# Pairwise products of 200 field vectors in fp32: TensorE's program as a loop over eight groups, and mixed rows moved by GpSimd and VectorE

## The chip, the cores and the metric

One NeuronCore of a Trainium2 chip. The metric is the device time of one execution in microseconds (us), the median of a few runs.

## The reference

Everything is fp32. There are 512 samples, each with 200 fields of 64 numbers, and a 64 x 64 weight matrix for every field.

```python
B, F, E = (256, 200, 64)            # r_feature is (512, 200, 64)
bilinear = jnp.einsum('bie,ied->bid', feature, weight)
out = jnp.einsum('bid,bjd->bij', bilinear, feature)
```

So every field i of a sample is first multiplied by its own matrix ("mixed"), and then the 200 x 200 products of mixed and plain field vectors of each sample are formed ("scores"). 82 MB of scores are written, 26 MB of features read.

## The kernel before

The samples are worked in 4 groups of 128. The 128 partitions hold two halves: partitions 0 to 63 the 64 numbers of one half of a group's samples, 64 to 127 those of the other half; the weights stand twice, once for each half (w_sb).

**Mixes.** A mix unit (L200) is 32 matmuls of a 64 x 64 weight with 64 moving columns (one column a sample) into a pair of PSUM banks, four tiles of 64 x 64 side by side in the array. The fields are taken in three chunks of 64 (four mix units each), and the last 8 fields ("tail") in a unit of their own (L217). In a mix unit one bank gets its result in the own half of the partitions, the other in the opposite half; ScalarE and VectorE copy them from PSUM into mixed (L293, and L291 for the bank that changes halves, in two copies of 64 partitions).

**Scores.** A score unit (L228) is 8 matmuls: for 8 samples the 64 mixed fields of a chunk are the stationary operand and all 200 plain fields of the sample, straight from x_sb, the moving one; again four tiles of 64 x 64 side by side. It fills a pair of banks, 128 x 800 numbers, which ScalarE (even units) or VectorE (odd units) copies to a slot of tile (L270); two units make an output of 128 x 1600 that SyncE (SP) sends (L154). tile has 6 slots. The tail's scores are two more units a group (L244) of 64 matmuls with 32 columns each.

**Order.** walk (L36) sets one order of units for all engines. The mix units of the next chunk stand between the score units of the present one. Four bank pairs go round, so a unit waits for the copy of the unit four before (wait_banks). TensorE, ScalarE, VectorE and SP each run their whole program unrolled. SP sends the outputs in order, and in between, one or two output issues apart, the loads of the next group: part 0 during chunk 0 into the other of two buffers, part 1 during the last chunk into the single buffer piece by piece (L155 to L162). GpSimd does one memset (L168).

In the recorded instructions every fp32 matmul shows as two MATMUL and two LDWEIGHTS.

## Time and profile before

| | |
|---|---|
| median of 3 runs | 349.12 us (348.49 to 352.26) |
| the profiled execution | 347.19 us, its span 345.4 us |
| TensorE (PE) busy | 250.5 us, 73% of the span |
| VectorE (DVE), ScalarE (ACT), GpSimd (POOL) busy | 148.4, 128.3 and 2.4 us |
| mean granted TensorE clock | 0.93 of full speed |
| moved by DMA | 115.70 MB, mean 335 GB/s |

The span is from the first to the last instruction of the profiled execution; what lies around it is 1.8 us. A line number in a row is that of the listing above. "<-" stands between a tile that is written and the one read, or ahead of what released an engine. PEld is the load of weights. "Issue" is time in which an engine waited for nothing that the profile shows. PEclk is given in tenths of full speed in the slices (9 is 0.9 or more), as a fraction in the windows; 1.00 is 2.4 GHz and half of it is 1.2 GHz.

### The profile page before, as it was taken

How to read it: one execution, taken by the hardware profiler on the slowest of the kernel's cores; microseconds unless marked ns; L12 is line 12 of the kernel's file. 1: busy time of each engine (PE TensorE's matmuls, PEld its weight loads, DVE VectorE, ACT ScalarE, POOL GpSimd, SP SyncE). 2: the span in 40 equal slices, each digit the busy share in tenths (PEclk: the TensorE clock that was granted, in tenths of full speed). 3: DMA queues.
4: the chain of work that ended last, by engine and by line, in shares of the span. 5: the costliest groups of instructions: out<-in, count | busy, mean ns of one | idle time of the engine just before them, and what ended most of it. 6: DMA issues, size and time to landing. Idle time of an engine off the chain costs nothing.

```text
span 345.4 us, 15674 instructions
## 1 busy us (share of the span) xinstructions
PE 250.5 (73%) x7296; PEld 221.2 (64%) x7296; DVE 148.4 (43%) x172; ACT 128.3 (37%) x177; POOL 2.4 (1%) x5
## 2 busy tenths in 40 slices
PE   0167679599967674969785967869985877987870
PEld 0156668378867573748775957748875766766760
DVE  0042455136634541605563553504653554635550
ACT  1032426045524422314452443403553444442540
POOL 2000000000000000000000000000000000000000
PEclk9987899899989988989998798989999999999995
DMA  7999998847999997757799999964899997746796
GB/s 302 423 426 423 400 368 280 331 193 289 351 409 399 395 388 261 236 242 291 300 374 418 395 366 421 306 286 194 335 373 390 407 386 312 289 199 260 284 408 286
DMA packets 21808, 115.70 MB, mean 335 GB/s; under 512 B 2416, under 2 KB 2416, under 8 KB 21360
## 3 DMA queue, kind: packets, MB, share of 16 engines
q1 hardware_dynamic: 21744, 114.70, 84.6%
q8 instruction: 58, 0.95, 1.1%
q14 instruction: 6, 0.05, 0.0%
HBM read 32.77 MB, written 81.92 MB: 332 GB/s over the span
## 4 chain that ended last, share of the span: by engine, by line
PE 72%; issue 19%; DMA 4%; DVE 1%; SPq 1%; ACT 1%
PE psum L238 46%; PE psum L210 16%; PE psum L255 9%; DMA w_sb<-w_dram 4%; PE psum L222 1%; DVE tile L270 1%; SPq L128 1%; ACT mixed L291 1%
## 5 line engine op out<-in xcount | busy, mean ns | idle before, releaser
L238 PE MATMUL psum<-x_sb,mixed 64*64 64x200 f32 x3072 | 173.2, 357 | 32.9 <-issue 29.5
L238 PEld LDWEIGHTS psum<-x_sb,mixed 64*64 64x64 f32 x3072 | 141.4, 143 | 49.5 <-issue 41.2
L270 DVE COPY tile<-psum 128x800 f32<-128x800 f32 x100 | 99.2, 992 | 141.2 <-PE psum L238 128.9
L270 ACT COPY tile<-psum 128x800 f32<-128x800 f32 x100 | 82.7, 827 | 117.2 <-PE psum L238 85.5
L210 PE MATMUL psum<-x_sb,w_sb 64*64 64x64 f32 x3072 | 67.7, 228 | 37.3 <-issue 21.3
L210 PEld LDWEIGHTS psum<-x_sb,w_sb 64*64 64x64 f32 x3072 | 65.6, 140 | 40.6 <-issue 39.5
L291 DVE COPY mixed<-psum 64x512 f32<-64x512 f32 x48 | 33.1, 689 | 28.2 <-PE psum L210 26.9
L291 ACT COPY mixed<-psum 64x512 f32<-64x512 f32 x48 | 27.9, 581 | 43.6 <-PE psum L210 43.0
L255 PE MATMUL psum<-x_sb,tails 64*32 64x200 f32 x1024 | 32.6, 377 | 13.0 <-issue 13.0
L255 PEld LDWEIGHTS psum<-x_sb,tails 64*32 64x32 f32 x1024 | 22.6, 115 | 21.7 <-issue 18.3
L293 ACT COPY mixed<-psum 128x512 f32<-128x512 f32 x24 | 14.1, 587 | 44.3 <-PE psum L210 44.2
L293 DVE COPY mixed<-psum 128x512 f32<-128x512 f32 x24 | 16.6, 692 | 17.6 <-PE psum L210 17.6
L222 PE MATMUL psum<-x_sb,w_sb 64*64 64x64 f32 x128 | 4.6, 220 | 0.5
L222 PEld LDWEIGHTS psum<-x_sb,w_sb 64*64 64x64 f32 x128 | 4.2, 132 | 0.9 <-issue 0.9
L300 ACT COPY tails<-psum 128x512 f32<-128x512 f32 x4 | 2.3, 586 | 0.3
L168 POOL MEMSET tails<- 128x2560 f32 x1 | 2.2, 2232 | 0.3 <-POOLq L324 0.3
L293 ACT ACT_TABLE_LOAD x1 | 1.3, 1283 | 0.7 <-PEq L324 0.7
L324 POOL MEMSET const-bfloat16-1.0<- 128x1 bf16 x1 | 0.1, 103 | 0.0
L324 POOL MEMSET const-uint8-127<- 128x1 uint8 x1 | 0.1, 102 | 0.0
L324 POOL MEMSET const-float32-0.0<- 128x1 f32 x1 | 0.1, 100 | 0.2 <-issue 0.2
L324 POOL MEMSET const-float32-1.0<- 128x1 f32 x1 | 0.1, 100 | 0.0
## 6 DMA issues: line engine op xcount, KB each, us to landing
out_dram<-tile SPq DMA_DIRECT2D x96, 800.0 KB, 6.3
x_sb<-x_dram SPq DMA_DIRECT2D x16, 800.0 KB, 8.7
x_sb<-x_dram SPq DMA_DIRECT2D x32, 400.0 KB, 7.7
w_sb<-w_dram SPq DMA_DIRECT2D x2, 2048.0 KB, 16.7
out_tail_dram<-tile SPq DMA_DIRECT2D x4, 800.0 KB, 4.5
w_sb<-w_dram SPq DMA_DIRECT2D x1, 2304.0 KB, 22.5
```

Source lines behind the costliest of these rows:

```text
L128: eng.dma_start(x_sb[:, 2 * (g % 2), quads], x[g, 0, :, quads]).then_inc(part0_loaded[g % 2], 16)
L168: nc.gpsimd.memset(tails[:], 0.0).then_inc(zeroed, 1)
L210: last = nc.tensor.matmul(psum[half_rows(h ^ swap), bank + swap, r * HALF_SAMPLES:(r + 1) * HALF_SAMPLES], w_sb[half_rows(h), field, :], x ...
L222: last = nc.tensor.matmul(psum[half_rows(h), n % BANK_PAIRS * 2, r * HALF_SAMPLES:(r + 1) * HALF_SAMPLES], w_sb[half_rows(h), TAIL_FIRST + ...
L238: last = nc.tensor.matmul(psum[half_rows(pair), n % BANK_PAIRS * 2 + h, a * FIELDS:(a + 1) * FIELDS], mixed[half_rows(h), (CHUNKS * g + c) ...
L255: last = nc.tensor.matmul(psum[tile4 * TAIL_TILE:(tile4 + 1) * TAIL_TILE, n % BANK_PAIRS * 2 + h, piece * FIELDS:(piece + 1) * FIELDS], we ...
L270: copy(tile[:, k % SLOTS, engine], psum[:, bank:bank + 2, 0:2 * FIELDS]).then_inc(copied[engine], 1)
L291: copy(to[half_rows(h)], source[half_rows(1 - h)]).then_inc(copied[engine], 1)
L293: copy(to, source).then_inc(copied[engine], 1)
L300: copy(tails[:, :, :, 0:TAIL], source).then_inc(copied[engine], 1)
L324: nc = bacc.Bacc("TRN2", target_bir_lowering=False, num_devices=1)
```

## The change

There are now 8 groups of 64 samples. The halves of the partitions no longer divide the samples but the fields: partitions 0 to 63 hold fields 0 to 103 of all 64 samples, partitions 64 to 127 fields 104 to 199 (96 fields and 8 rows of zeros). The weights are loaded once, split alike.

A mix unit is 32 matmuls as before (two units have 16, the last 8); its results go to made, one ScalarE copy a unit (L299). To score, all 200 mixed fields of a sample must stand in both halves. So made is copied to mixed in eight steps of 8 samples: VectorE copies all partitions straight across into fields 0 to 99 (L309), and GpSimd, in two copies of 64 partitions, the rows that change halves into fields 100 to 199 (L195). GpSimd also copies x_in, which lies field by field, to x_now, which lies sample by sample (L188), in eight steps.

A score unit has 2 samples: x_now with 104 or 96 columns is the stationary operand, the 200 mixed fields the moving one (L230), so two matmuls, one a half, stand side by side. ScalarE copies 5 units of 8, VectorE 3. Two units make an output of 96 x 1600 and one of 8 x 800 (L158, L159); tile has 4 slots. The tails are gone.

x_in is a single buffer: SP loads the next group right after the first output of a group (in the first group after the fourth), when GpSimd has copied all of x_in (x_placed) and the mixes have read it. TensorE's program is a loop of 7 rounds (L251), one group's 32 score units and the next group's 8 mix units, with the semaphore values in registers; the last group stands behind the loop. The other engines stay unrolled.

```diff
-GROUPS = 4
-HALVES = 2
-QUADS = BATCH // GROUPS // 4
-HALF_SAMPLES = 2 * QUADS
+GROUPS, SLOTS = 8, 64
+MAIN, REST = 96, 8
+TOP = MAIN + REST
+PIECES = 3
+PIECE = MAIN // PIECES
+MIX = [(16 * m, 8, 2) for m in range(5)] + [(80, 4, 2), (88, 4, 2), (MAIN, 4, 1)]
+MIXES = len(MIX)
+MADE = FIELDS // 2
...
+MIX_AFTER = (7, 9, 12, 14, 17, 20, 22, 24)
+STEPS = 8
+STEP_SLOTS = SLOTS // STEPS
+STEP_UNITS = STEP_SLOTS // UNIT_SAMPLES
+NEXT_STEPS_AFTER = {28: 0, 30: 1}
+STEPS_AFTER = {STEP_UNITS * n + 2: n + 2 for n in range(STEPS - 2)}
+POOL_STEPS = [("x", c) for c in range(6)] + [("rows", 0), ("x", 6), ("rows", 1), ("x", 7)]
+POOL_STEPS += [("rows", c) for c in range(2, STEPS)]
+TILE_UNITS = 2
+TILES = SCORES // TILE_UNITS
+TILE_SLOTS = 4
...
+def engine_of(u):
+    return 0 if u % 2 == 0 or u % 8 == 7 else 1
...
-def build(nc, x, weight, out, out_tail):
-    sb = lambda name, shape: nc.alloc_sbuf_tensor(name, shape, F32)
-    w_sb = sb("w_sb", [128, FIELDS, EMB])
-    x_sb = sb("x_sb", [128, 3, QUADS, PART, 2])
-    mixed = sb("mixed", [128, 2, QUADS, CHUNK, 2])
+    w_sb = sb("w_sb", [128, TOP, EMB])
+    x_in = sb("x_in", [128, TOP, SLOTS])
+    x_now = sb("x_now", [128, SLOTS, TOP])
+    made = sb("made", [128, 2, SLOTS, MADE])
+    mixed = sb("mixed", [128, SLOTS, FIELDS])
+    tile = sb("tile", [128, TILE_SLOTS, 2, TILE_UNITS, UNIT_SAMPLES * FIELDS])
...
         def _(sp):
...
+            for p in range(PIECES + 1):
+                load_x(0, p)
+                load_w(p)
+            for g in range(GROUPS):
+                for t in range(TILES):
+                    k = g * TILES + t
+                    s = k % TILE_SLOTS
+                    for u in range(TILE_UNITS * t, TILE_UNITS * (t + 1)):
+                        e = engine_of(u)
+                        sp.wait_ge(copied[e], COPIES[NUMBER["score", g, u]][e])
+                    sp.dma_start(out[g, t], tile[0:MAIN, s]).then_inc(slot_out[s], 16)
+                    sp.dma_start(out_rest[g, t], tile[MAIN:TOP, s, 0]).then_inc(slot_out[s], 16)
+                    if g + 1 < GROUPS and t == (3 if g == 0 else 0):
+                        sp.wait_ge(x_placed, STEPS * (g + 1))
+                        sp.wait_ge(unit_ready, NUMBER["mix", g, MIXES - 1] + 1)
+                        for p in range(PIECES + 1):
+                            load_x(g + 1, p)
...
         def _(pool):
-            nc.gpsimd.memset(tails[:], 0.0).then_inc(zeroed, 1)
+            nc.gpsimd.memset(x_in[half_rows(1), MAIN:TOP, :], 0.0).then_inc(zeroed, 1)
+            pool.wait_ge(zeroed, 1)
+            for g in range(GROUPS):
+                for p in range(PIECES + 1):
+                    pool.wait_ge(x_loaded[p], 16 * (g + 1))
+                for step in POOL_STEPS:
+                    what, c = step
+                    slots = slice(c * STEP_SLOTS, (c + 1) * STEP_SLOTS)
+                    if step == ("rows", 0):
+                        pool.wait_ge(copied[0], COPIES[NUMBER["mix", g, MIXES - 1]][0])
+                    if g > 0 and what == "x":
+                        pool.wait_ge(unit_ready, NUMBER["score", g - 1, (c + 1) * STEP_UNITS - 1] + 1)
+                    if g > 0 or crossed_before(step):
+                        pool.wait_ge(crossed, 2 * (STEPS * g + crossed_before(step)))
+                    if what == "x":
+                        nc.gpsimd.tensor_copy(
+                            x_now[:, slots, :], x_in[:, :, slots].rearrange("p f s -> p s f")).then_inc(x_placed, 1)
+                    else:
+                        pool.wait_ge(x_placed, STEPS * g + min(STEPS, 6 + c))
+                        for h in range(2):
+                            if h == 1:
+                                pool.wait_ge(crossed, 2 * (STEPS * g + c) + 1)
+                            nc.gpsimd.tensor_copy(mixed[half_rows(h), slots, MADE:FIELDS],
+                                                  made[half_rows(1 - h), g % 2, slots, :]).then_inc(crossed, 1)
...
         def _(pe):
...
+            def mix(n, m):
+                first, width, banks = MIX[m]
+                bank = n % BANK_PAIRS * 2
+                for r in range(width):
+                    for swap in range(2):
...
+                            last = nc.tensor.matmul(
+                                psum[half_rows(h ^ swap), bank + (swap if banks == 2 else 0),
+                                     r * SLOTS:(r + 1) * SLOTS],
+                                w_sb[half_rows(h), field, :], x_in[half_rows(h), field, :],
+                                start=True, stop=True)
+                last.then_inc(unit_ready, 1)
-                wait_banks(n)
-                if t == 0 and u == 0:
-                    wait_copies(NUMBER["mix", g, c, MIX_UNITS - 1])
-                if c == 0 and u == 0:
-                    wait_part1(g, t)
-                for a in range(2):
-                    quad = 4 * t + 2 * u + a
-                    for pair in range(2):
-                        for h in range(HALVES):
-                            last = nc.tensor.matmul(
-                                psum[half_rows(pair), n % BANK_PAIRS * 2 + h, a * FIELDS:(a + 1) * FIELDS],
-                                mixed[half_rows(h), (CHUNKS * g + c) % 2, quad, :, pair],
-                                x_sample(g, h, quad, pair), start=True, stop=True)
+            def score(n, u):
+                bank = n % BANK_PAIRS * 2
+                for a in range(UNIT_SAMPLES):
+                    slot = UNIT_SAMPLES * u + a
+                    for h, rows in enumerate((TOP, MAIN)):
+                        last = nc.tensor.matmul(
+                            psum[0:rows, bank + h, a * FIELDS:(a + 1) * FIELDS],
+                            x_now[half_rows(h), slot, 0:rows], mixed[half_rows(h), slot, :], start=True, stop=True)
+                last.then_inc(unit_ready, 1)
+            def wait_step(g, u):
+                if u % STEP_UNITS == 0:
+                    steps = u // STEP_UNITS + 1
+                    pe.wait_ge(x_placed, g * STEPS + steps)
+                    pe.wait_ge(mixed_placed, g * STEPS + steps)
+                    pe.wait_ge(crossed, g * (2 * STEPS) + 2 * steps)
+            with pe.Fori(0, GROUPS - 1) as g:
+                x_there = 16 * g + 32
+                pe.compute_val(x_there)
+                for kind, to, k in order(1):
+                    n = NUMBER[kind, to, k]
+                    (free, value), = banks_free(n, g)
+                    pe.compute_val(value)
+                    if kind == "mix":
+                        pe.wait_ge(w_loaded[piece_of(k)], 16)
+                        pe.wait_ge(free, value)
+                        pe.wait_ge(x_loaded[piece_of(k)], x_there)
+                        mix(n, k)
+                    else:
+                        pe.wait_ge(free, value)
+                        wait_step(g, k)
+                        score(n, k)
...
         def copies(eng, copy, engine):
...
+                    eng.wait_ge(slot_out[k % TILE_SLOTS], 32 * (k // TILE_SLOTS))
+                bank = n % BANK_PAIRS * 2
+                copy(tile[0:TOP, k % TILE_SLOTS, :, u % TILE_UNITS, :],
+                     psum[0:TOP, bank:bank + 2, 0:UNIT_SAMPLES * FIELDS]).then_inc(copied[engine], 1)
...
+            def place(g, c):
+                if c == 0:
+                    eng.wait_ge(copied[0], COPIES[NUMBER["mix", g, MIXES - 1]][0])
+                if g > 0:
+                    eng.wait_ge(unit_ready, NUMBER["score", g - 1, (c + 1) * STEP_UNITS - 1] + 1)
+                slots = slice(c * STEP_SLOTS, (c + 1) * STEP_SLOTS)
+                copy(mixed[:, slots, 0:MADE], made[:, g % 2, slots, :]).then_inc(mixed_placed, 1)
+            if engine == 0:
+                for m in range(MIXES):
+                    mix(0, m)
+            else:
+                for c in NEXT_STEPS_AFTER.values():
+                    place(0, c)
+            for g in range(GROUPS):
+                for kind, to, k in order(g):
+                    if kind == "mix":
+                        if engine == 0:
+                            mix(to, k)
+                        continue
+                    if engine_of(k) == engine:
+                        score(g, k)
+                    if engine == 1 and k in STEPS_AFTER:
+                        place(g, STEPS_AFTER[k])
+                    if engine == 1 and k in NEXT_STEPS_AFTER and g + 1 < GROUPS:
+                        place(g + 1, NEXT_STEPS_AFTER[k])
```

How the instructions stand. First TensorE in the middle of a group, before. L238 is a score matmul, L210 a mix matmul, L255 one of the tail; x_sb is the input, mixed the mixed fields.

```order
L238 MATMUL psum<-x_sb,mixed 64x200 [waits copied_dve]
L238 MATMUL psum<-x_sb,mixed 64x200 x7
L238 MATMUL psum<-x_sb,mixed 64x200 [waits copied_act]
L238 MATMUL psum<-x_sb,mixed 64x200 x7
L255 MATMUL psum<-x_sb,tails 32x200 [waits copied_act,copied_dve,zeroed]
L255 MATMUL psum<-x_sb,tails 32x200 x63
L238 MATMUL psum<-x_sb,mixed 64x200 [waits copied_dve,copied_act]
L238 MATMUL psum<-x_sb,mixed 64x200 x7
L238 MATMUL psum<-x_sb,mixed 64x200 [waits copied_act]
L238 MATMUL psum<-x_sb,mixed 64x200 x7
L210 MATMUL psum<-x_sb,w_sb 64x64 [waits part1_loaded3,part1_loaded2,part1_loaded4,part1_loaded1,part1_loaded5,part1_loaded0,part1_loaded6,w_loaded2,part1_loaded7,part0_loaded0,copied_dve]
L210 MATMUL psum<-x_sb,w_sb 64x64 x31
```

After, units 6 and 7 of a group, the first mix unit of the next group, and unit 8. L230 is a score matmul, L218 one of a mix; L257, L239 and L241 are register and wait instructions.

```order
L230 MATMUL psum<-mixed,x_now 104x200 [waits copied_dve]
L230 MATMUL psum<-mixed,x_now 96x200
L230 MATMUL psum<-mixed,x_now 104x200
L230 MATMUL psum<-mixed,x_now 96x200
L257 REGISTER_ALU
L218 MATMUL psum<-x_in,w_sb 64x64 [waits x_loaded0,copied_act,w_loaded0]
L218 MATMUL psum<-x_in,w_sb 64x64 x31
L257 REGISTER_ALU
L239 REGISTER_ALU [waits copied_dve]
L241 REGISTER_ALU [waits mixed_placed,x_placed]
L230 MATMUL psum<-mixed,x_now 104x200 [waits crossed]
```

The first mix unit now waits for x_loaded0, the first piece of the next group, which before was loaded one chunk or more earlier; between the units stand register instructions.

SP (SyncE), before, at the end of a group: outputs (L154) and the loads of the next group (L132).

```order
L154 DMA out_dram<-tile 128x1600 [waits copied_dve,copied_act] x5
L154 DMA out_tail_dram<-tile 128x1600 [waits copied_dve,copied_act]
L154 DMA out_dram<-tile 128x1600 [waits copied_dve,copied_act] x4
L132 DMA x_sb<-x_dram 128x800
L154 DMA out_dram<-tile 128x1600 [waits copied_dve,copied_act]
L132 DMA x_sb<-x_dram 128x800
L154 DMA out_dram<-tile 128x1600 [waits copied_dve,copied_act]
```

After, at the start of the second group: the outputs are L158 and L159, the loads L137 and L139.

```order
L158 DMA out_dram<-tile 96x1600 [waits copied_act]
L159 DMA out_rest_dram<-tile 8x800
L158 DMA out_dram<-tile 96x1600 [waits copied_dve,copied_act]
L159 DMA out_rest_dram<-tile 8x800
L137 DMA x_in<-x_dram 128x2048 [waits unit_ready,x_placed]
L137 DMA x_in<-x_dram 128x2048 x2
L139 DMA x_in<-x_rest_dram 64x512
L158 DMA out_dram<-tile 96x1600 [waits copied_dve,copied_act]
L159 DMA out_rest_dram<-tile 8x800
```

The loads stood singly between outputs; now all of a group's loads stand behind its first output, behind a wait for GpSimd (x_placed) and TensorE (unit_ready).

GpSimd, before, from its start to its end.

```order
L166 UNCONDITIONAL_BRANCH [waits barrier_Pool_Activation_PE_DVE_SP_gather]
L168 MEMSET tails 128x2560
L134 UNCONDITIONAL_BRANCH
```

After, in the second group, from the end of the x steps on (L188 copies x_in to x_now, L195 rows that change halves).

```order
L188 COPY x_now<-x_in 128x832 [waits crossed,unit_ready] x5
L195 COPY mixed<-made 64x8x100 [waits x_placed,crossed,copied_act]
L195 COPY mixed<-made 64x8x100 [waits crossed]
L188 COPY x_now<-x_in 128x832 [waits crossed,unit_ready]
L195 COPY mixed<-made 64x8x100 [waits x_placed,crossed]
L195 COPY mixed<-made 64x8x100 [waits crossed]
L188 COPY x_now<-x_in 128x832 [waits crossed,unit_ready]
L195 COPY mixed<-made 64x8x100 [waits x_placed,crossed]
L195 COPY mixed<-made 64x8x100 [waits crossed]
```

Before, GpSimd had no copy at all; now each of its copies waits for the one before, and the x steps also for the score units of the group before (unit_ready).

## Rows read from the trace of the kernel before

**Rows 1.** The page: busy shares; 40 equal slices of PE (tenths) and DMA (GB/s).

```profile
PE 250.5 (73%) x7296; PEld 221.2 (64%) x7296; DVE 148.4 (43%) x172; ACT 128.3 (37%) x177; POOL 2.4 (1%) x5
...
PE   0167679599967674969785967869985877987870
...
GB/s 302 423 426 423 400 368 280 331 193 289 351 409 399 395 388 261 236 242 291 300 374 418 395 366 421 306 286 194 335 373 390 407 386 312 289 199 260 284 408 286
```

**Rows 2.** The page: chain that ended last.

```profile
PE 72%; issue 19%; DMA 4%; DVE 1%; SPq 1%; ACT 1%
```

**Rows 3.** Waits of TensorE: who waited for what, us in total, times, longest.

```profile
PE psum L238 <- issue: 29.5, 17, 4.5
PE psum L210 <- issue: 21.3, 14, 3.1
PE psum L210 <- DMA w_sb<-w_dram: 16.0, 1, 16.0
PE psum L255 <- issue: 13.0, 6, 3.9
```

**Rows 4.** The page: instruction queue; issues, us to landing; then all x_sb loads.

```profile
q8 instruction: 58, 0.95, 1.1%
...
out_dram<-tile SPq DMA_DIRECT2D x96, 800.0 KB, 6.3
x_sb<-x_dram SPq DMA_DIRECT2D x16, 800.0 KB, 8.7
...
DMA to landing us min/median/max: 4.4/7.8/18.2
```

**Rows 5.** The page: groups of instructions.

```profile
L270 DVE COPY tile<-psum 128x800 f32<-128x800 f32 x100 | 99.2, 992 | 141.2 <-PE psum L238 128.9
L270 ACT COPY tile<-psum 128x800 f32<-128x800 f32 x100 | 82.7, 827 | 117.2 <-PE psum L238 85.5
...
L168 POOL MEMSET tails<- 128x2560 f32 x1 | 2.2, 2232 | 0.3 <-POOLq L324 0.3
...
L324 POOL MEMSET const-bfloat16-1.0<- 128x1 bf16 x1 | 0.1, 103 | 0.0
```

**Rows 6.** The chain in order of time, 150 to 165 us: start, us, what.

```profile
154.61 0.95 PE psum L210 x59
155.56 1.43 PE psum L238 x28
156.99 3.02 PE psum L255 x116
...
161.60 1.04 PE psum L210 x60
```

**Rows 7.** Timeline of the last stretch: start, us, what.

```profile
322.13 0.83 ACT L270 COPY tile<-psum 128x800 f32<-128x800 f32 x1 [1.73 <-PE psum L238]
...
333.62 0.83 ACT L270 COPY tile<-psum 128x800 f32<-128x800 f32 x1 [0.62 <-PE psum L238]
334.33 0.99 DVE L270 COPY tile<-psum 128x800 f32<-128x800 f32 x1 [0.44 <-PE psum L238]
```

**Rows 8.** Windows: busy of each engine, PEclk, DMA share, GB/s.

```profile
26.50:335.40 308.90, 243.77 (x7040) 214.69 (x7040) 144.23 (x166) 123.53 (x170) 0.00 (x0) 0.94 0.85 332
...
26.00:31.70 5.70, 5.12 (x89) 4.37 (x91) 1.14 (x2) 2.03 (x3) 0.00 (x0) 0.60 1.02 432
321.00:334.40 13.40, 13.15 (x288) 12.53 (x288) 8.00 (x9) 7.40 (x9) 0.00 (x0) 1.00 0.83 335
```

**Rows 9.** Timeline of the start.

```profile
0.73 2.06 SPq L128 DMA_DIRECT2D x_sb<-x_dram  x4
...
15.99 5.43 PE L210 MATMUL psum<-x_sb,w_sb 64*64 64x64 f32 x221 [15.99 <-DMA w_sb<-w_dram]
...
26.58 4.91 PE L238 MATMUL psum<-x_sb,mixed 64*64 64x200 f32 x64 [1.43 <-ACT mixed L291]
```

**Rows 10.** Waits of SyncE.

```profile
SPq L164 <- DMA out_dram<-tile: 9.1, 1, 9.1
```

More of the change, by code:

```diff
@@ L39, in half_rows, with crossed_before @@
+POOL_STEPS = [("x", c) for c in range(6)] + [("rows", 0), ("x", 6), ("rows", 1), ("x", 7)]
[3 more added lines that the diff above has]
+TILE_SLOTS = 4
+def crossed_before(step):
+    return sum(what == "rows" for what, _ in POOL_STEPS[:POOL_STEPS.index(step)])
 def half_rows(h):
     return slice(h * EMB, (h + 1) * EMB)
[L43 to L69 removed]
@@ new lines, in engine_of, with fields_by_position @@
+def engine_of(u):
+    return 0 if u % 2 == 0 or u % 8 == 7 else 1
+def fields_by_position():
+    made = [[], []]
+    for first, width, banks in MIX:
+        if first == MAIN:
+            for h in range(2):
+                made[h] += range(first + h * width, first + (h + 1) * width)
+        else:
+            for bank in range(banks):
+                for h in range(2):
+                    a = h * TOP + first + bank * width
+                    made[h ^ bank] += range(a, a + width)
+    return [made[h] + made[1 - h] for h in range(2)]
@@ new lines, in order @@
+def order(g):
+    for u in range(SCORES):
+        yield "score", g, u
+        if u in MIX_AFTER and g + 1 < GROUPS:
+            yield "mix", g + 1, MIX_AFTER.index(u)
+def count_copies():
+    copies, number = [], {}
+    units = [("mix", 0, m) for m in range(MIXES)] + [unit for g in range(GROUPS) for unit in order(g)]
+    a = d = 0
+    for n, (kind, g, k) in enumerate(units):
+        engine = 0 if kind == "mix" else engine_of(k)
+        a, d = a + (engine == 0), d + (engine == 1)
+        copies.append((a, d))
+        number[kind, g, k] = n
+    return copies, number
@@ L335 @@
[L335 to L342 removed]
+    r = run_bass_kernel_spmd(nc, [inputs], core_ids=[0]).results[0]
```

285 lines of the change are left out of this document (84 added, 201 removed).

## The prediction

> **What bounds the kernel now.** I read the page's busy line and its slices first, then the chain of waits, the waits of TensorE, the groups by line, clean stretches in the timeline, and the DMA part. TensorE is busy in 7 to 9 tenths of nearly every slice while VectorE and ScalarE stay near half, and the DMA rows are high but uneven, 193 to 426 GB/s [rows 1]. The chain that ended last runs 72% over TensorE and 19% over "issue" [rows 2]: 0.192 x 345.4 = 66 us in which TensorE waited for nothing that the profile shows. TensorE's own waits put 29.5, 21.3 and 13.0 us of such time before its three kinds of work, together 64 us, in 37 pieces of up to 4.5 us [rows 3]. Only instruction delivery fits: the instruction queue moved 58 packets, 0.95 MB [rows 4], for 2 x 7,296 TensorE instructions [rows 1], so 16 KB and about 250 instructions a packet; the pauses fall more thickly around mixes and tails, which use up instructions fastest. So TensorE bounds the kernel, partly starved of instructions; the DMA engines come second.
>
> **TensorE's work.** One unit is what one pair of banks takes. In a complete stretch a mix unit (64 recorded matmuls) stands for about 1.0 us (0.95 and 1.04), two score units for 1.43 us, a tail unit for 3.02 us [rows 6]; the last stretch, at clock 1.00, has ScalarE's copies from 322.13 to 333.62 in eight steps, 1.44 us for two score units, too [rows 7]. Before: 192 x 0.72 + 50 x 1.0 + 8 x 3.0 = 212 us. The chain shows 249 (72%), a factor of 1.17: cold stretches after pauses (clock 0.94 in the middle and 0.60 in one stretch, where the first four score units took 4.9 us instead of 2.9 [rows 8, 9]) and small handovers.
> After: a score unit holds 2 samples x 2 halves = 4 matmuls instead of 8, but they are 104 or 96 columns wide, so only two stand side by side instead of four. Half the matmuls at half the concurrency: 0.72 us again, but 256 units instead of 192. The tails go (-24 us). The mixes keep 3,200 recorded matmuls, 50 us. Sum 184 + 50 = 234, 22 us more than before. Of this 6 us (the first group's mixes) lie in the start. For the other 228 I take a factor of 1.12, between 1.05 (the last stretch, without pauses, is at 1.00; I allow 5% for handovers) and 1.17 (as before), since one kind of pause goes and another comes (below): 255 us, bounds 239 to 267.
>
> **Instruction pauses.** The body of the new loop is 128 score and 200 mix matmuls, 1,312 recorded instructions; by 65 bytes each 85 KB. If it stays in the engine, the 66 us go; if it is fetched again in every round, they stay in part. No row shows which. I take the first, since the body is a tenth of what the program was, and give the other as a rival. No row prices the register instruction that now stands ahead of each unit; the smallest instruction on the page takes 0.10 us [rows 5]. I cost them at 0, covered by matmuls already queued; uncovered, 0.1 us x 320 units = 32 us, of which the range holds half.
>
> **Loads of the next group.** Before, x of the next group is spread over output issues a chunk or more ahead, and TensorE's waits show no x load at all [rows 3]. Now x_in is single: SP issues all four loads after tile 0 of the group. That is 2 units, 1.4 us, a copy of 1.0 us and an issue, so 2.8 us into the group. The old 800 KB loads took a median of 8.7 us from issue to landing [rows 4]; the first mix wants its piece after eight units, 5.8 us in. Wait: 2.8 + 8.7 - 5.8 = 5.7 us; with the fastest landings (4.4 us) 1.4 us. I take 5 x 7 groups = 35 us, bounds 10 to 45. Queued behind the waiting matmul are all later score units; the copies run dry after 4 bank pairs. Behind SP's wait for x_placed stand the outputs; that wait ends once GpSimd has moved x step 7, which itself waits for the last score unit of the group before.
>
> **GpSimd and VectorE.** Per group GpSimd gets 8 copies of 832 elements and 16 of 800. The only row of it is the memset, 2,560 elements in 2,232 ns, 0.87 ns an element, write only [rows 5]: at this floor 8 x 0.73 + 16 x 0.70 = 17 us a group. If reading takes as long again, 34 us. TensorE's group is (23 + 6.2) x 1.12 + 5 = 38 us, so up to 34 it is hidden but for the start. I take 1.4 us for an x step (its reads are strided) and 1.0 for a row copy with its semaphore: 27 us. VectorE: 12 x 0.99 + 8 x 0.9 = 19 us; ScalarE: 20 x 0.83 + about 6.6 = 23 us a group [rows 5]: both hidden.
>
> **DMA.** An output of 800 KB takes 819,200 B / 426 GB/s = 1.92 us at the best slice rate [rows 1, 4]. The new one has 96 partitions: 1.44 us by its bytes, 1.92 if its time goes by the row alone, whatever the partitions. The eight-partition output adds about 0.1. With x (3.3 MB, 7.8 us) a group costs 33 to 39 us, against 38 for TensorE. I take 33, hidden.
>
> **Start and end.** Before, the loads start at 0.7 us, w lands at 15.9 and scoring starts at 26.6 [rows 9]. Now 6.6 MB instead of 5.4 go first: 13.0 us x 6.6 / 5.4 + 2.8 = 18.8 us. Then GpSimd moves six x steps (8.4 us) and the first pair of rows (2.0) before scoring: 29.5 us, bounds 25 to 34. The end before is 10 us from the last copy at 335.3, nine of them SP's wait for outputs [rows 7, 8, 10]; the last group now loads nothing, so less stands in the queue: 5 us.
>
> **Sum.** 29.5 + 255 + 35 + 5 = 324.5 us of span. The profiled run took 347.2 us for a span of 345.4, so 326 us; the median of the runs is 349.1, 1.9 us above it, and I give 327 us for the measured time. What a measurement tells from no change is about 1%, the spread of the three runs (348.5 to 352.3): faster means under 345.6, slower over 352.6.
>
> **Rivals.** *The loop is fetched anyway.* 10,496 instructions against 14,592 leave 0.72 x 66 = 47 us of pauses; score instructions are used up half as fast, which speaks for less, some overlap the x waits, but each of seven jumps back may miss for as long as the longest pauses, 3 to 4.5 us [rows 3]. Net 30 us: 357, slower. For it: the pauses show that the engine does not get far ahead. The Trainium skill ("Runtime: NRT & Kernel Launch", Instruction fetch mechanics) says that a taken branch to a target outside the present window forces a fetch; it also gives TensorE room for 2,048 instructions, which this body would fit. No run here shows a branch yet.
> *GpSimd sets the pace* (the case on the other side). The place is the chain rows step, x step, rows step; it decides from about 38 us a group. At 2.0 us an x step and 1.55 a row copy (read and write in series, a strided read dearer still, waits on its own semaphores) it is 41 us: 18.8 + 8 x 41 + 8 for the last step and output = 355, and 357 measured. For it: every copy waits for the one before, and there is no copy row. Against: the memset's 0.87 ns. The Trainium skill ("GPSIMD Engine Reference", Performance pitfalls for Q7 kernels) states about 2.9 cycles an element for reads with a step over 8 bytes and 1.9 otherwise, at 1.2 GHz: an estimate of 2.0 and 1.27 us, 36 us a group, on the edge; the memset agrees only with its faster figure of about 1 cycle.
> *The 96-partition output costs what a 128-partition one does.* Then 39 us of DMA a group, no longer hidden: 29.5 + 7 x 40 + 31 + 3 = 343.5, measured 346, within 1%. 
>
> **Chances.** Forecast 0.46, with 315 to 348 as its own range: 0.42 faster, 0.04 same. DMA 0.16: 0.06 faster, 0.08 same, 0.02 slower. GpSimd 0.13 and fetched loop 0.21: together 0.31 slower, 0.01 same, 0.02 faster. Better than 315 on the low bounds (short x waits, clock near 1): 0.04. In all faster 0.54, same 0.13, slower 0.33. The range goes from 310 (x waits of 2 us) to 362 (above both slow cases).
>
> **What would show it.** Right: few "issue" pauses and an instruction queue well under 0.5 MB; score units 0.72 us apart at full clock; TensorE waiting about 5 us for x_in before the first mix of each group; GpSimd under 30 us a group; scoring from about 29.5 us. Wrong: 0.7 MB of instructions with a pause at each round (first rival); matmuls waiting for GpSimd's row copies (second); copies waiting for output slots while output rates stay near 320 GB/s (third); or score units clearly over 0.72 us at clock 1.00, which would upset the main term.

## The result, and the profile after

The changed kernel takes 373.77 us (median of 4 runs, 369.68 to 379.08); the kernel before took 348.81 us beside it. Ratio 1.059, 95% interval 1.046 to 1.071: 6% slower, where 327 us was forecast, and outside the range. In some executions the whole program runs 2% longer at the same work, here in two of the four (377.47 and 379.08 us against 369.68 and 370.08), so the ratios leave such executions out and differences to the changed kernel are counted below from 370 us. The profiled execution took 369.68 us with a span of 367.9 us, against a sum of 324.5 us: 43.4 us to be explained.

First the page of the changed kernel; it answers to [rows 1, 2, 4]: busy shares, slices, queues and the chain by engine and by line.

```profile
PE 271.6 (74%) x5248; PEld 238.1 (65%) x5248; DVE 134.9 (37%) x160; ACT 178.2 (48%) x225; POOL 237.1 (64%) x197
...
PE   1755349982999659982999469981999549997860
...
DMA  8900986998999999999999999999989999999997
GB/s 316 394 7 0 282 353 186 292 300 290 373 331 309 301 360 364 303 302 338 377 317 320 299 367 365 291 314 357 355 284 303 294 353 351 312 297 324 313 297 249
...
q1 hardware_dynamic: 20992, 111.43, 88.6%
q8 instruction: 10, 0.16, 0.2%
...
DMA 37%; PE 31%; SPq 14%; POOL 6%; ACT 6%; issue 3%; DVE 1%; ACTq 0%; POOLq 0%; DVEq 0%
DMA out_rest_dram<-tile 27%; PE psum L230 22%; PE psum L218 9%; SPq L158 6%; DMA x_in<-x_dram 6%; ACT tile L286 5%; DMA x_in<-x_rest_dram 4%; POOL x_now L188 4%; SPq L159 3%; SPq L137 3%; POOL mixed L195 2%; SPq L139 1%; ACT made L299 1%; DVE tile L286 1%; SPq L144 0%
```

The bound has moved. Before, the chain ran 72% over TensorE and 4% over DMA; now 37% over DMA, and SP's own issuing is another 14%. The row that says most is the pair DMA and GB/s: from the eleventh slice on the DMA engines show 9 tenths nearly everywhere, yet they move 249 to 338 GB/s in 20 of these 30 slices and 351 to 377 in the other ten. The DMA row of before shows which slices were full then:

```profile
DMA  7999998847999997757799999964899997746796
```

The slices with a 9 there moved 366 to 426 GB/s [rows 1], all but two (351 and 306). Engines that are as full and move less point at inefficient transfers, not at a lack of work.

The waits, all engines (who waited for what, us in total, times, longest), answer to [rows 3]:

```profile
ACT tile L286 <- DMA out_rest_dram<-tile: 66.0, 62, 2.3
PE psum L218 <- DMA x_in<-x_dram: 54.2, 7, 10.3
...
DVE tile L286 <- DMA out_rest_dram<-tile: 40.9, 28, 2.6
...
PE psum L230 <- POOL mixed L195: 9.7, 3, 6.6
```

TensorE's 64 us of waits for "issue" before matmuls are gone, 1.7 us in three pieces are left; in the chain "issue" fell from 19 to 3%. In their place ScalarE and VectorE wait 66.0 and 40.9 us for output slots, which can hold TensorE back through the bank pairs, and TensorE waits 54.2 us, seven times, for the next group's x.

One group's period can be read in the chain in order of time (start, us, what). The first two lines end the wait for x of one group, the later ones that of the group two further on:

```profile
167.77 6.25 DMA x_in<-x_dram
174.16 1.99 PE psum L218 x64
...
179.37 2.20 PE psum L230 x18
181.57 1.09 PE psum L218 x64
...
195.33 4.07 DMA out_rest_dram<-tile
...
249.07 7.45 DMA x_in<-x_dram
256.52 0.14 issue
256.66 1.98 PE psum L218 x64
```

From 174.16 to 256.66 are two groups, 41.25 us each; the forecast had (255 + 35) / 8 = 36.25. All seven of these waits end 40.3 to 42.3 us apart. At clock 1.00 three score units take 2.20 us, 0.733 each (forecast 0.72), and a mix unit 1.09 (1.0): TensorE's work was sized well. Right after a wait for x it is slower: the mix unit there takes 1.98 us, at a granted clock of 0.50 (256.70 to 260.50 us), that is the lower level, 1.2 GHz. So each wait for x costs about 0.9 us more in that unit alone.

Two stretches of outputs alone, the two groups together, and the stretch behind the last wait above, as windows (busy time of each engine, clock, DMA share, GB/s):

```profile
146.00:156.00 10.00, 10.00 (x224) 8.63 (x222) 3.94 (x5) 7.92 (x12) 4.90 (x3) 1.00 0.95 303
187.00:197.00 10.00, 10.00 (x222) 8.63 (x220) 4.24 (x6) 7.62 (x11) 5.07 (x4) 1.00 0.94 311
174.16:256.66 82.50, 66.00 (x1312) 57.35 (x1313) 33.60 (x40) 44.14 (x56) 59.86 (x50) 0.91 0.97 334
256.70:260.50 3.80, 3.80 (x76) 3.52 (x78) 0.00 (x0) 1.23 (x2) 1.07 (x2) 0.50 1.00 316
```

An output pair is 96 x 6400 + 8 x 3200 = 640,000 bytes, so 2.11 and 2.06 us at these rates. Sixteen of them and 3.3 MB of x at 0.4 MB/us (8.1 us; an estimate from the loads at the start, 394 GB/s in the second slice) make 41.1 to 41.9 us: the measured period. TensorE is busy throughout the two short stretches, in which it fills the output slots faster than they are emptied, but only for 66.0 of the 82.5 us of two groups; the DMA engines have a share of 0.97 there. The DMA engines set the pace.

### The profile page after: what moved, and what is told of

The parts are those of the page before. It is cut to its first block, busy times and chain, and to the rows that moved or that the text cites. A ratio compares the mean times of both kernels' runs of the same rounds, so it can differ in the third digit from the quotient of the medians.

```text
span 367.9 us, 12472 instructions
## 1 busy us (share of the span) xinstructions
PE 271.6 (74%) x5248; PEld 238.1 (65%) x5248; DVE 134.9 (37%) x160; ACT 178.2 (48%) x225; POOL 237.1 (64%) x197
## 3 DMA queue, kind: packets, MB, share of 16 engines
q1 hardware_dynamic: 20992, 111.43, 88.6%
HBM read 29.49 MB, written 81.92 MB: 303 GB/s over the span
## 4 chain that ended last, share of the span: by engine, by line
DMA 37%; PE 31%; SPq 14%; POOL 6%; ACT 6%; issue 3%; DVE 1%; ACTq 0%; POOLq 0%; DVEq 0%
DMA out_rest_dram<-tile 27%; PE psum L230 22%; PE psum L218 9%; SPq L158 6%; DMA x_in<-x_dram 6%; ACT tile L286 5%; DMA x_in<-x_rest_dram 4%; POOL x_now L188 4%; SPq L159 3%; SPq L137 3%; POOL mixed L195 2%; SPq L139 1%; ACT made L299 1%; DVE tile L286 1%; SPq L144 0%
## 5 line engine op out<-in xcount | busy, mean ns | idle before, releaser
L230 PE MATMUL psum<-mixed,x_now 64*104 64x200 f32 (+1 forms) x2048 | 204.2, 349 | 17.4 <-POOL mixed L195 9.7
L230 PEld LDWEIGHTS psum<-mixed,x_now 64*104 64x104 f32 (+1 forms) x2048 | 172.6, 171 | 34.5 <-ACT tile L286 10.2
L286 ACT COPY tile<-psum 104x800 f32<-104x800 f32 x160 | 129.2, 829 | 102.4 <-DMA out_rest_dram<-tile 66.0
L188 POOL COPY x_now<-x_in 128x832 f32<-128x832 f32 x64 | 113.3, 1787 | 98.1 <-DMA x_in<-x_rest_dram 47.2
L286 DVE COPY tile<-psum 104x800 f32<-104x800 f32 x96 | 95.1, 991 | 197.6 <-PE psum L230 156.5
L195 POOL COPY mixed<-made 64x800 f32<-64x800 f32 x128 | 123.1, 962 | 10.6 <-ACT made L299 1.6
L218 PE MATMUL psum<-x_in,w_sb 64*64 64x64 f32 x3200 | 74.1, 246 | 68.0 <-DMA x_in<-x_dram 54.2
L218 PEld LDWEIGHTS psum<-x_in,w_sb 64*64 64x64 f32 x3200 | 65.5, 157 | 84.2 <-issue 84.2
L299 ACT COPY made<-psum 128x1024 f32<-128x1024 f32 (+1 forms) x64 | 53.1, 829 | 79.4 <-PE psum L218 79.4
L309 DVE COPY mixed<-made 128x800 f32<-128x800 f32 x64 | 45.5, 713 | 25.9 <-ACT made L299 25.9
```

The source lines that it names most:

```text
L188: nc.gpsimd.tensor_copy(x_now[:, slots, :], x_in[:, :, slots].rearrange("p f s -> p s f")).then_inc(x_placed, 1)
L195: nc.gpsimd.tensor_copy(mixed[half_rows(h), slots, MADE:FIELDS], made[half_rows(1 - h), g % 2, slots, :]).then_inc(crossed, 1)
L218: last = nc.tensor.matmul(psum[half_rows(h ^ swap), bank + (swap if banks == 2 else 0), r * SLOTS:(r + 1) * SLOTS], w_sb[half_rows(h), fie ...
L230: last = nc.tensor.matmul(psum[0:rows, bank + h, a * FIELDS:(a + 1) * FIELDS], x_now[half_rows(h), slot, 0:rows], mixed[half_rows(h), slot ...
L286: copy(tile[0:TOP, k % TILE_SLOTS, :, u % TILE_UNITS, :], psum[0:TOP, bank:bank + 2, 0:UNIT_SAMPLES * FIELDS]).then_inc(copied[engine], 1)
L299: copy(made[:, g % 2, :, at:at + width * banks].rearrange("p s (k r) -> p s k r", k=banks), psum[:, bank:bank + banks, 0:width * SLOTS].re ...
```

## The experiments

### The transfer by itself

A program that only sends: stages of 12 outputs of 6,400 bytes a row, from 128 rows, 96 rows from partition 0, 96 from 32, the two by turns, 64 rows from 0, 64 from 0 and 64 by turns, 104 rows, and 96 rows followed by 8.

```python
for i, kinds in enumerate(stages):
    for k in range(N):
        ...
        sp.dma_start(to, tile[a:a + rows, k % 2, 0:width]).then_inc(done[i], 16)
    ...
    sp.wait_ge(done[i], 16 * total)
```

> Eight stages of 12 output DMAs each, rows of 6400 B (the rows of 8 partitions: 3200 B), and nothing else: 128 rows; 96 rows from partition 0; 96 from 32; 96 from 0 and from 32 by turns; 64 from 0; 64 from 0 and from 64 by turns; 104 rows; 96 rows with the 8 rows behind each. Port theory (the lower 64 partitions drain through half of the ways out): the stages of 128 and 96 rows take the same 1.93 us a DMA, 64 rows from 0 take it too, 64 by turns about 1.0 us, 96 by turns 1.45 us. Byte theory (only bytes count): 1.93, 1.45, 1.45, 1.45, 0.97, 0.97 us. Theory of the small DMA: the last stage is clearly over the second, by 0.2 us or more a pair.

The windows lie inside the stages, in the order above (no compute; clock, DMA share, GB/s):

```profile
14.00:24.00 10.00, 0.00 (x0) 0.00 (x0) 1.00 1.02 416
32.00:36.00 4.00, 0.00 (x0) 0.00 (x0) 1.00 1.00 317
62.00:70.00 8.00, 0.00 (x0) 0.00 (x0) 1.00 0.99 322
90.00:98.00 8.00, 0.00 (x0) 0.00 (x0) 1.00 1.01 336
118.00:124.00 6.00, 0.00 (x0) 0.00 (x0) 1.00 1.01 212
140.00:150.00 10.00, 0.00 (x0) 0.00 (x0) 1.00 0.95 260
164.00:174.00 10.00, 0.00 (x0) 0.00 (x0) 1.00 0.82 298
196.00:206.00 10.00, 0.00 (x0) 0.00 (x0) 1.00 0.92 280
```

128 rows: 819,200 B / 416 = 1.97 us. 96 rows: 614,400 / 317 = 1.94 us. 64 rows: 409,600 / 212 = 1.93 us. The upper 32 rows, and even the upper 64, save nothing; the engines are full all the while (share 1.00), they only move less. (These are the fullest stretches of each stage; 96 rows fall to 303 GB/s at a share of 0.96 later in theirs.) The Trainium skill ("SBUF — State Buffer", Door 1: The DMA port swizzle) says that one half of the partitions reaches only half of the ports, and by that rule a full half sets the time: the traces agree for transfers of one placement (1.91 to 1.97 us whether one half or both are full). By turns from the two ends, two transfers in flight should fill each other's gaps; they do so only in small part (336 instead of 317, 260 instead of 212): 1.83 and 1.58 us where this theory expected 1.45 and 1.0. 104 rows (665,600 B) take 2.23 us, more than 128, at a DMA share of 0.82; the pair of 96 and 8 rows takes 640,000 / 280 = 2.29 us.

### All 128 rows, and no 8-row output

```diff
-                    sp.dma_start(out[g, t], tile[0:MAIN, s]).then_inc(slot_out[s], 16)
-                    sp.dma_start(out_rest[g, t], tile[MAIN:TOP, s, 0]).then_inc(slot_out[s], 16)
+                    sp.dma_start(out[g, t], tile[:, s]).then_inc(slot_out[s], 16)
```

> Each output sends all 128 partitions of its tile slot (24 of them zeros) in one DMA, and the DMA of 8 rows is gone; 105 MB written instead of 82. Port theory: 128 rows cost what 96 do, and the small DMA goes: as fast as the changed kernel or up to 15 us faster, 355 to 372 us, at some 380 GB/s. Byte theory: a third more time for the outputs that now bound the kernel, 273 us x 1.28, so over 420 us. Theory that four slots and their latency bound it: the same time within 5 us.

376.78 us, ratio 1.082 (1.070 to 1.094). It writes 104.86 MB instead of 81.92, 28% more, and is only 7 us, 2%, slower than the changed kernel. That is above the 355 to 372 us of the port theory, but far from the 420 of the byte theory:

```profile
GB/s 318 379 7 10 362 327 265 399 401 379 398 403 409 386 392 366 388 410 367 416 341 387 381 401 359 365 414 384 398 337 389 375 399 410 344 389 410 403 411 258
...
DMA 65%; PE 13%; ACT 9%; issue 6%; POOL 4%; SPq 1%; ACTq 1%; POOLq 0%
```

Compare this GB/s row with that of the changed kernel: the slices of 300 are 400 now, in nearly the same time. 24 rows more of zeros cost almost nothing, so 96 rows are paid nearly as 128. A bound by the four slots and their latency, the third theory, isn't excluded by this run (the same time within 5 us was expected of it); the run with the same bytes, below, keeps the four slots and speaks against it.

### The 96-row output alone

```diff
-                    sp.dma_start(out_rest[g, t], tile[MAIN:TOP, s, 0]).then_inc(slot_out[s], 16)
+                    if g == GROUPS - 1 and t == TILES - 1:
+                        sp.dma_start(out_rest[g, t], tile[MAIN:TOP, s, 0]).then_inc(slot_out[s], 16)
```

> The 127 first DMAs of 8 rows are left out (rows 96 to 103 of the scores are not written). Port theory: 1.93 us instead of some 2.1 a tile at most, so 350 to 370 us. Theory of the small DMA (its own fixed cost and its place in the queue are what makes a tile 2.1 us): under 340 us. Theory that late loads of x_in set the time: no change, 370 us.

369.79 us, ratio 1.061 (1.049 to 1.074), no different from the changed kernel within the intervals. The small output is not what costs, nor are its 127 issues on SP. In the windows at 146 and 187 us the 96-row outputs alone go at 284 and 280 GB/s, 2.16 and 2.19 us each, no faster than the pairs (the port theory had 1.93).

### The same bytes on all rows

The clean test of the cause: as many bytes a tile as the changed kernel sends, but 5,000 of each of 128 rows instead of 6,400 of 96 and 3,200 of 8.

```diff
-                    sp.dma_start(out[g, t], tile[0:MAIN, s]).then_inc(slot_out[s], 16)
-                    sp.dma_start(out_rest[g, t], tile[MAIN:TOP, s, 0]).then_inc(slot_out[s], 16)
+                    row = tile[:, s].rearrange("p a b c -> p (a b c)")
+                    to = out[g, t].rearrange("p a b c -> p (a b c)")
+                    sp.dma_start(to[:, 0:1250], row[:, 0:1250]).then_inc(slot_out[s], 16)
```

> The changed kernel with outputs of all 128 rows in one DMA, of which each sends only its first 1250 of 1600 numbers (128 x 1250 x 4 = 640,000 B a tile, exactly the bytes of the changed kernel's 96-row and 8-row DMAs together); no 8-row DMA; 24 of the rows are zeros, and the last 350 numbers of each row's scores are not written. Theory 'a DMA from SBUF takes the time of its fullest rows, and 96 rows cost what 128 do': a tile takes 1.97 x 1250 / 1600 = 1.54 us (1.97 us is what the DMA-only stage of 128 rows measured), a group's DMA work 16 x 1.54 + 8.1 = 33 us, less than the 36 us that TensorE and the x chain need, so the DMA engines no longer set the pace: 332 to 345 us, and over 390 GB/s in stretches full of outputs. Theory 'only the bytes count, 0.3 MB/us is what these outputs get beside the work of the engines': a tile stays at 2.1 us and the kernel at 368 to 378 us.

336.71 us, ratio 0.977 (0.968 to 0.986), as expected if the rows count: 33 us less than the changed kernel, by the spans too (367.9 and 334.6), 29 by the ratios, at the same 111.4 MB. Its queue, chain and two windows of it (the first in the middle of a group, the second late in the run, with outputs alone):

```profile
q1 hardware_dynamic: 23040, 111.42, 85.1%
...
PE 47%; POOL 23%; DMA 19%; issue 4%; ACT 3%; SPq 1%; ACTq 0%; POOLq 0%
PE psum L233 32%; PE psum L221 16%; POOL x_now L191 12%; POOL mixed L198 12%; DMA x_in<-x_dram 11%; DMA x_in<-x_rest_dram 5%; DMA out_dram<-tile 3%; ACT tile L291 2%; ACT made L304 1%; SPq L144 0%; ACTq L130 0%; SPq L137 0%; SPq L160 0%; POOLq L189 0%; POOLq L194 0%
```

```profile
220.00:224.00 4.00, 4.00 (x58) 3.64 (x56) 1.16 (x2) 2.84 (x5) 3.35 (x3) 1.00 0.79 320
...
320.00:324.00 4.00, 3.67 (x41) 2.91 (x39) 1.93 (x3) 2.82 (x4) 2.55 (x3) 1.00 1.00 401
```

Where outputs queue up they go at 401 GB/s, 1.60 us each; elsewhere the DMA engines have gaps (share 0.79). Chain: TensorE 47%, outputs 3% where they had 27%. It computes all scores and isn't a usable kernel, since it drops the last 350 numbers of each row; but it shows that the way the bytes lie on the rows, not their number, made the changed kernel slow. It also sends one DMA a tile instead of two; the run above, with the 96-row output alone, shows that this gains nothing.

### Outputs of a quarter, and x loaded once

```diff
-                    sp.dma_start(out[g, t], tile[0:MAIN, s]).then_inc(slot_out[s], 16)
-                    sp.dma_start(out_rest[g, t], tile[MAIN:TOP, s, 0]).then_inc(slot_out[s], 16)
+                    sp.dma_start(out[g, t, :, 0, 0], tile[0:MAIN, s, 0, 0]).then_inc(slot_out[s], 16)
+                    sp.dma_start(out_rest[g, t, :, 0], tile[MAIN:TOP, s, 0, 0]).then_inc(slot_out[s], 16)
```

> Only the first unit's first half of each output is sent (a quarter of the bytes; the rest of the scores is not written), all instructions of TensorE, ScalarE, VectorE and GpSimd as in the changed kernel. If outputs whose 96 rows cost as much as 128 are what the forecast of 327 us left out: 315 to 335 us. If TensorE, GpSimd or the start are slower than forecast on their own: over 345 us.

331.14 us (one run): with the outputs' cost all but gone, the forecast of 327 is met within 1.3%. So the rest of the sum was sound in total.

```profile
q1 hardware_dynamic: 20992, 50.80, 45.8%
...
PE 52%; POOL 24%; DMA 16%; issue 4%; ACT 3%; SPq 1%; ACTq 0%; POOLq 0%
```

The other half of the DMA work, the x loads of groups 1 to 7, left out (the waits for them with it):

```diff
-                        for p in range(PIECES + 1):
-                            load_x(g + 1, p)
+                        pass
```

> The x loads of groups 1 to 7 are left out (all groups are computed from the first group's features), outputs as in the changed kernel. Outputs alone, at the 2.2 us of a pair of 96 and 8 rows, need 128 x 2.2 = 282 us from about 33 us on: 318 us with the end, if they bound it then. If TensorE's own pace sets it: 33 + 228 x 1.05 + 5 = 277 to 290 us.

320.41 us (one run), within 1% of the 318 that 128 outputs at 2.2 us give. But the agreement is in part luck, for the outputs aren't the only bound here. From 100 to 330 us the DMA share is 0.87, and the chain is led by GpSimd:

```profile
POOL 37%; DMA 25%; PE 13%; ACT 7%; issue 7%; SPq 6%; DVE 2%; ACTq 1%; POOLq 0%
```

So with x for nothing the outputs and GpSimd's copies hold this kernel about equally, and what the outputs alone would take, the run doesn't show.

### Moving the x loads, and fewer slots

Loads ahead of the group's first output instead of behind it (here and with 128-row outputs):

```diff
                 for t in range(TILES):
+                    if g + 1 < GROUPS and t == (3 if g == 0 else 0):
+                        sp.wait_ge(x_placed, STEPS * (g + 1))
+                        sp.wait_ge(unit_ready, NUMBER["mix", g, MIXES - 1] + 1)
+                        for p in range(PIECES + 1):
+                            load_x(g + 1, p)
```

> SP issues the next group's four x loads ahead of the output of the same place instead of behind it. In the changed kernel's trace GpSimd had ended x step 7 at 164.5 us and the loads were issued at 167.8, since the output ahead of them waited for a slot. Theory that TensorE's wait for x_in (54 us in 7 pieces) is on the path: each piece shortens by about 3 us plus the output no longer ahead in the queue, so 20 to 35 us less, 340 to 352 us. Theory that the DMA engines alone bound the kernel (they do the same work in another order): 365 to 375 us.

> Both: outputs of whole 128 partitions without the DMA of 8 rows, and the x loads ahead. If the DMA engines are the bound, 128 x 1.97 + 29.5 MB at 0.41 MB/us = 324 us of work, plus some 12 us idle at the start and 5 at the end: about 342. If the order of x loads and slots matters alone, as the run with the loads ahead, within 5 us.

375.35 us (ratio 1.078, 1.070 to 1.086) and 377.77 us (1.082, 1.074 to 1.091), 5 and 8 us above the changed kernel. The first, its waits:

```profile
DVE tile L285 <- DMA out_rest_dram<-tile: 103.1, 32, 13.5
ACT tile L285 <- DMA out_rest_dram<-tile: 83.3, 55, 5.5
...
PE psum L217 <- DMA x_in<-x_dram: 39.0, 7, 9.2
```

TensorE waits 15 us less for x, and the copies 80 us more for slots (two engines, partly at the same time); the total doesn't fall. Here the order of the queue's work only chose who waits.

The second run missed its forecast of 342 us by 36. From 100 to 330 us its DMA engines have a share of 0.96:

```profile
100.00:330.00 230.00, 188.10 (x3630) 160.69 (x3628) 89.07 (x108) 120.02 (x152) 150.17 (x123) 0.91 0.96 380
```

They are full, but at 380 GB/s, where the forecast had 410 to 416 from the program that only sends: 128 MB from the start of scoring on are 337 us at the one rate and 310 at the other. And at the start they stand nearly idle for two slices (6 and 22 GB/s), 19 us, for which 12 were forecast. So the DMA engines still set the time; what was wrong is the rate, and why it is lower inside the kernel stays open.

One load behind each of four outputs:

```diff
+                    p = t - (3 if g == 0 else 0)
+                    if g + 1 < GROUPS and 0 <= p <= PIECES:
+                        if p == 0:
+                            sp.wait_ge(x_placed, STEPS * (g + 1))
+                            sp.wait_ge(unit_ready, NUMBER["mix", g, MIXES - 1] + 1)
+                        load_x(g + 1, p)
```

> The four x loads of the next group no longer stand in one burst of 3.3 MB: one stands behind each of four outputs. Same bytes, same DMAs. Theory of the burst (the 8 us of loads hold back the outputs behind them, all four slots fill, and copies and TensorE stop; the DMA engines then run short later in the group): 10 to 25 us less, 350 to 364 us, with TensorE's wait for x_in and the copies' waits for slots both down. Theory that the DMA engines' total work alone sets the time: 368 to 376 us.

> The same with outputs of whole 128 partitions and no DMA of 8 rows. If, once the burst is gone, the cost of an output sets the pace, the 0.2 to 0.3 us that the 8-row DMA adds to each tile show: 10 to 20 us less than with the loads between alone, 335 to 350 us, which would be level with or below the kernel before. If not, within 4 us of it.

384.31 us (ratio 1.107, 1.096 to 1.118) and 389.3 us (1.122, 1.117 to 1.127): both misses, outside every range that was expected of them: my idea that the burst of loads does harm fell. The profile of the first suggests why:

```profile
q1 hardware_dynamic: 20992, 111.43, 85.9%
```

```profile
PE psum L218 <- DMA x_in<-x_dram: 67.8, 8, 11.3
...
ACT tile L286 <- DMA out_rest_dram<-tile: 40.6, 38, 1.9
```

The waits for slots shrank, 66.0 to 40.6 us for ScalarE, but those for x grew from 54.2 to 67.8, and the DMA share fell from 88.6 to 85.9%, the same work in a longer span. My reading, which no further run tests: x has one buffer, so its loads are on the path from the last x step to the next mix; the longer they take, the longer TensorE makes no outputs, and the DMA engines run dry.

Three output slots instead of four:

```diff
-TILE_SLOTS = 4
+TILE_SLOTS = 3
```

> Three output slots instead of four, all else as in the changed kernel. If the four slots are a bound together with the burst: each burst starves TensorE by one tile (1.5 to 2 us) more in 7 groups and outputs overlap less, so 15 us or more above the changed kernel, over 385 us. If only DMA rates count: within 5 us of 372.

385.25 us (one run): a slot less costs about 15 us. So slots help to carry outputs over the wait for x. More than four weren't tried; by how much they would shorten the changed kernel is open.

### TensorE unrolled

The loop replaced by its seven rounds, everything else as in the changed kernel:

```diff
-            with pe.Fori(0, GROUPS - 1) as g:
-                x_there = 16 * g + 32
-                pe.compute_val(x_there)
-                for kind, to, k in order(1):
+            for group in range(GROUPS - 1):
+                for kind, to, k in order(group):
...
```

> The TensorE program is written out instead of looped, all else as in the changed kernel. If the loop took the pauses away: the instruction queue is back to 0.7 MB or more, issue pauses of some 20 to 45 us come back, and the time rises by 5 to 30 us to 375 to 400 us (part of it hidden behind the outputs). If the register instructions and the jumps cost more than the fetches: 360 to 370 us.

384.12 us, ratio 1.107 (1.093 to 1.121), 13 us more than the changed kernel, 17 by the ratios. Its instruction queue, and TensorE's waits for "issue":

```profile
q8 instruction: 41, 0.67, 0.7%
...
PE psum L218 <- issue: 6.3, 7, 1.7
PE psum L230 <- issue: 1.6, 2, 1.4
```

Against 10 packets and 0.16 MB with the loop. The loop does what it is for, but it removes far less than the 64 us of pauses before: written out, the new program has only 7.9 us of them before matmuls, where 20 to 45 were expected, and 1.7 with the loop. So most of the old pauses went with something else in the change. A likely reason, not shown, is that instructions can arrive while TensorE waits for x (57.2 us in this run). The 6 us of pauses don't account for all of the 13 either.

## Why the prediction was wrong, step by step

**The step that failed** is in the part on DMA: "The new one has 96 partitions: 1.44 us by its bytes, 1.92 if its time goes by the row alone, whatever the partitions ... I take 33, hidden." The right end of that pair was the upper one. Sent by itself the 96-row output takes 1.94 us, in the kernel a pair of outputs 2.06 to 2.11, and a group's DMA work is 41 us, not 33. It isn't hidden but sets the period (41.25 us). The last copy ends at 360.6, so from the start of scoring at 32.15 it is 328.5 us where the forecast had 255 + 35 = 290: 38.5 of the 43.4 us missing, about 5 us a group. Scoring starts 2.7 us later than forecast, and after the last copy come 7.3 us instead of 5. The run with the same bytes on 128 rows takes the rival "only bytes count" away: it is 33 us shorter in its span.

**The rival** that held this mechanism had a chance of 0.16 and gave 346 us. Its sign, copies that wait for output slots while the rates stay near 320 GB/s, is what the trace shows (66.0 and 40.9 us of such waits, 303 and 311 GB/s). It was undersized by 24 us. Its groups are 40 us, which is 16 x (1.92 + 0.1) + 7.8 (the upper figure of the DMA part, 39, leaves the small output out), at the best rate of the old slices; 41.25 was measured. Its last group is 31 where 16 outputs at 2.06 to 2.11 us are 33 to 34, its start 29.5 for 32.15, its end 3 for 7.3. These make 18 of the 24. From the same rows a higher figure was to be had: 400 GB/s, about what the full slices before show [rows 1], is 2.05 us a tile, 16 x 2.05 + 8.1 = 41 us a group, and 29.5 + 7 x 41 + 33 + 3 = 352.5 us, which would still have been too low. Its place as the side case was the error of judgment: the price at stake (6 us a group by its own figures) was known, no row of before excluded it, and a DMA share of 0.85 in the middle [rows 8] left no room for it.

**The instruction pauses** went as forecast in size: 10 packets instead of 58, and 1.7 us of "issue" before matmuls instead of 64. Seven times 85 KB would be 0.6 MB, and 0.16 MB were moved, which is what the body and the last group behind it take once (2 x 85 KB). So the body stays in the engine. By the rule that the first rival quoted (the Trainium skill, "Runtime: NRT & Kernel Launch", Instruction fetch mechanics: a taken branch to a target outside the window forces a fetch) there would be a pause each round if the body's start had left the window; the trace shows none, and the same section's room of 2,048 instructions for TensorE, which holds this body, fits. But that the loop is what saves the 66 us, as the forecast had it, isn't borne out: the unrolled run has 7.9. Of the register instructions' cost no row shows anything; no run takes them away alone.

**TensorE's units** were right to 2% (0.733 for 0.72 us) and 9% (1.09 for 1.0).

**x loads.** Forecast 5 us a group, 35 us; measured 54.2, 7.7 each, which is 19 of the 38.5 us. Where the outputs are cheap, it is 30.4 us (quarter) and 32.0 us (same bytes, all rows): the estimate holds for a queue that isn't full, and the rest comes from the same wrong step. How is read from the timeline: the first output and the issue of the loads are late, because the copies wait for slots, and the loads go in beside queued outputs.

**GpSimd.** Forecast 1.4 us an x step and 1.0 us a row copy, 27 us a group; measured, in the changed kernel:

```profile
L188 POOL COPY x_now<-x_in 128x832 f32<-128x832 f32 x64 | 113.3, 1787 | 98.1 <-DMA x_in<-x_rest_dram 47.2
...
L195 POOL COPY mixed<-made 64x800 f32<-64x800 f32 x128 | 123.1, 962 | 10.6 <-ACT made L299 1.6
```

(8 x 1.787 + 16 x 0.962) = 29.7 us a group, below the 38 us at which the second rival would have decided. In the changed kernel it is hidden for the most part (6% of the chain); in the runs where the outputs are cheap it takes 23 to 24%. It would be among the next bounds, with TensorE. In the start it shows: the first six x steps took 10.0 us instead of 8.4, a part of the 2.7 us.

## What to carry to other kernels

Price a DMA out of SBUF by the bytes of one row, not by all its bytes: between 64 and 128 rows of 6,400 B took the same 1.9 to 2.0 us wherever one half of the partitions was full (104 rows, at 2.23 us, stand outside this). A layout that leaves the upper rows of a tile unused pays for them all the same, and a change that trims the partitions to the data saves no time. Where DMA engines are 85% full, give every transfer whose shape changes a measured rate before any gain elsewhere is counted; a gain on TensorE is worth only what the second resource leaves. And once a queue is full, moving transfers in it moves the wait from one engine to another, as the two runs with the loads first show.

## What the runs showed of the hardware that was not expected

Transfers from opposite ends of the partitions, in flight together, hardly fill each other's gaps: 96 rows by turns 336 GB/s against 317 (+6%), 64 rows by turns 260 against 212 (+23%). The Trainium skill ("SBUF — State Buffer", Can I just issue two DMAs to hit both halves?) gives 6% for tiles at 0 and 64; here that is too little for the 64-row pair, though far nearer than double. 104 rows in one DMA are worse than 128 (2.23 against 1.97 us), with a DMA share of 0.82. That is the share of 13 engines out of 16, and 104 is 8 x 13: it looks as if the rows were dealt to 13 engines, which is inferred from this one stage.

GpSimd and VectorE copies between SBUF tiles disturb each other. Minimum, median and maximum of one (ns, then first and last start in us), for GpSimd's two kinds and VectorE's:

```profile
L188 POOL COPY x_now<-x_in x64: 1575/1646/2707, 20.2 to 329.1; 128x832 f32<-128x832 f32 x64
```

```profile
L195 POOL COPY mixed<-made x128: 848/850/2070, 30.3 to 344.4; 64x800 f32<-64x800 f32 x128
L309 DVE COPY mixed<-made x64: 560/567/1947, 25.9 to 349.4; 128x800 f32<-128x800 f32 x64
```

Each kind has a sharp median and single ones of 1.6 to 3.4 times that. The trace shows where they stand. Of GpSimd's 128 row copies the 104 that no VectorE copy into mixed overlaps took 848 to 852 ns, the 24 others 1,017 to 2,070. Of its 64 x steps the 41 without such an overlap took at most 1,665 ns. Those with an overlap took up to 2,707. VectorE's 64 copies into mixed took 566 to 569 ns in the 23 cases where GpSimd didn't copy, up to 1,947 in the others. VectorE's copies from PSUM took 978 to 993 ns all the same, 77 of the 96 beside a copy of GpSimd. So the slow ones stand only where both engines copy from SBUF to SBUF. The Trainium skill ("SBUF — State Buffer", A bandwidth-pool intuition that's wrong) says that GpSimd and a VectorE copy of this kind fully block each other for as long as one lasts, which fits this pattern; how long each was blocked, no row shows.

Open is why a tile of 128 rows takes 2.05 us inside the kernel (400 GB/s, as many of its slices have) and 1.97 alone, and what in the taking of turns gives the small gain.
